# A transformer layer's feed-forward tail: where the squared norms are clamped, where the Newton steps stand, and whether TensorE takes norms or scores first

## The reference, cut to what matters

```python
q = (hidden_states @ Wq + bq).reshape(B, S, H, QD)        # 8 heads of 64
q = (q - mean) / jnp.sqrt(var + EPS_BN) * bn_gamma + bn_beta
q0 = _l2norm(q[..., :HALF])                               # x / max(|x|, 1e-12)
q1 = _l2norm(q[..., HALF:])
s0 = jnp.einsum('bshq,kq->bshk', q0, _l2norm(sub_key0))   # 32 keys
s1 = jnp.einsum('bshq,kq->bshk', q1, _l2norm(sub_key1))
ts0, ti0 = jax.lax.top_k(s0, DTK)                         # 4 of 32, twice
ts1, ti1 = jax.lax.top_k(s1, DTK)
...                                                       # 16 pairs, softmax weights w
eh = jax.nn.gelu(jnp.einsum('bshkd,bsd->bshk', expert_down[idx], hidden_states), approximate=False)
out = jnp.einsum('bshko,bshk->bso', expert_up[idx], eh * w)
```

## Time and profile before

| | |
|---|---|
| median of 3 runs | 424.44 us (423.92 to 425.02) |
| profiled execution, its own time | 424.07 us |
| span of its instructions | 422.1 us |
| PE busy | 398.3 us (94%) |
| DVE busy | 298.3 us (71%) |
| ACT busy | 239.9 us (57%) |
| POOL busy | 208.2 us (49%) |
| granted TensorE clock, mean | 0.992 |

### The profile page before, as it was taken

The page is one execution under the profiler, slowest core; times in us unless marked ns, Lnnn a source line. Parts: engine busy times, 40 slices in busy tenths (PEclk is TensorE's granted clock), DMA queues, the critical chain, the costliest instruction groups (busy, mean ns, idle before and its releaser), DMA issues. The chain is left out here.

```text
span 422.1 us, 7841 instructions
## 1 busy us (share of the span) xinstructions
PE 398.3 (94%) x2569; PEld 366.2 (87%) x2569; DVE 298.3 (71%) x1112; ACT 239.9 (57%) x527; POOL 208.2 (49%) x195
## 2 busy tenths in 40 slices
PE   2999999987999999999999999999999988999877
PEld 2788888866899999999999999998787978999866
DVE  5889677667556575475764655557595999898996
ACT  3687656314655455565554544443465878777363
POOL 2588999931814234332343312000120757989894
PEclk9999999999999999999999999999999997999999
DMA  8700222002322123212222200000000000000101
GB/s 250 263 2 2 78 77 77 6 0 78 107 79 76 53 79 101 58 50 55 78 76 58 78 2 2 0 2 1 27 0 1 2 3 1 26 27 26 39 26 62
DMA packets 19991, 21.36 MB, mean 51 GB/s; under 512 B 3180, under 2 KB 16624, under 8 KB 19952
## 3 DMA queue, kind: packets, MB, share of 16 engines
q1 hardware_dynamic: 18832, 19.96, 15.7%
q10 hardware_dynamic: 1120, 0.92, 0.8%
HBM read 18.78 MB, written 2.10 MB: 49 GB/s over the span
## 5 line engine op out<-in xcount | busy, mean ns | idle before, releaser
L971 PE MATMUL att_pA<-context_cNh,att_pTh 128*128 128x256 f32 (+1 forms) x208 | 62.6, 301 | 1.0 <-DVE att_pTl L869 1.0
L972 PE MATMUL att_pA<-context_cNl,att_pTh 128*128 128x256 f32 (+1 forms) x208 | 58.4, 281 | 0.0
L973 PE MATMUL att_pA<-context_cNh,att_pTl 128*128 128x256 f32 (+1 forms) x208 | 58.1, 279 | 0.0
L869 DVE TENSOR_TENSOR att_pTl<-att_pR,att_pTh 128x512 fp32r<-128x512 f32 x64 | 37.4, 586 | 26.7 <-ACT att_pTh L786 26.5
L1166 POOL TENSOR_TENSOR ffn_prod<-ffn_first,ffn_near 128x1024 f32<-128x1024 f32 (+1 forms) x29 | 54.2, 1887 | 2.1 <-DVE ffn_first L1559 2.1
L888 DVE TENSOR_REDUCE att_mx<-keep_pQ 128x1 f32<-128x402 f32 x64 | 35.6, 568 | 25.4 <-PE keep_pQ L77 25.3
L776 POOL TENSOR_TENSOR context_cTl<-keep_raw,context_cTh 128x512 fp32r<-128x512 f32 (+1 forms) x24 | 23.1, 981 | 47.8 <-ACT context_cTh L800 47.8
L776 POOL TENSOR_TENSOR context_cNl<-keep_raw,context_cNh 128x512 fp32r<-128x512 f32 (+1 forms) x21 | 25.1, 1211 | 41.8 <-ACT context_cNh L800 41.8
L971 PEld LDWEIGHTS att_pA<-context_cNh,att_pTh 128*128 128x128 f32 (+1 forms) x208 | 39.1, 188 | 2.2 <-DVE att_pTl L869 1.4
L972 PEld LDWEIGHTS att_pA<-context_cNl,att_pTh 128*128 128x128 f32 (+1 forms) x208 | 39.3, 189 | 0.0
L973 PEld LDWEIGHTS att_pA<-context_cNh,att_pTl 128*128 128x128 f32 (+1 forms) x208 | 39.2, 188 | 0.0
(11 more groups left out here) (302 smaller groups left out, 1153.2 us busy)
## 6 DMA issues: line engine op xcount, KB each, us to landing
keep_raw<-in_ctxT SPq DMA_DIRECT2D x24, 256.0 KB, 2.6
keep_raw<-in_ctx SPq DMA_DIRECT2D x24, 256.0 KB, 2.6
out<-keep_x SPq DMA_DIRECT2D x16, 128.0 KB, 1.7
keep_x<-in_x SPq DMA_DIRECT2D x3, 512.0 KB, 9.1
gru_wout<-in_W_out SPq DMA_DIRECT2D x1, 512.0 KB, 8.6
keep_raw<-in_fWq SPq DMA_DIRECT2D x2, 256.0 KB
keep_raw<-in_ctxT SPq DMA_DIRECT2D x8, 32.5 KB, 3.6
keep_raw<-in_ctx SPq DMA_DIRECT2D x4, 65.0 KB
```

Source lines behind the costliest of these rows:

```text
L869: dve.tensor_tensor(to, bank, half(it, 0, n)[0].bitcast(F32), ALU.subtract).then_inc(bank_free, 1)
L971: pe.matmul(pA[:, 0:D], l[0], r[0], start=(kt == 0), stop=False)
L972: pe.matmul(pA[:, 0:D], l[0], r[1], start=False, stop=False)
L973: last = pe.matmul(pA[:, 0:D], l[1], r[0], start=False, stop=(kt == CT - 1))
```

## The change

- The clamp leaves VectorE. ScalarE computes `over = Relu(n - eps^2)` from PSUM and then `nroot = Sqrt(over + eps^2)`, which is the same number. Both take their constant from a small tile (`eps2`), as a bias.
- A Sqrt of one column (`eps1`) stands ahead of the wait for TensorE's norms; the table load goes with it.
- The Newton step is written with the factor -0.5 taken into the keys (`keyT`), and the steps of batches 1 to 4 now stand between the match-replaces of `remove`: behind head 1 the reciprocal, behind heads 3, 5 and 7 the other three. Before, those of batches 1 and 2 stood behind the whole `remove` and those of 3 and 4 between MAX8.
- TensorE takes `norms` ahead of `scores` in every other pass.
- GpSimd sets the two constants at the start of the stage.

```diff
@@ gpsimd
+                for n, v in enumerate((-NORM_EPS ** 2, NORM_EPS ** 2)):
+                    pool.memset(eps2[:, n:n + 1], v).then_inc(const_ready, 1)
@@ scalar
                 def norm_roots(k):
-                    act.wait_ge(n2_ready, k + 1)
-                    m = len(BATCHES[k]) * PER * HALVES
-                    act.activation(nroot[:, 0:m], n2[:, 0:m], ACT.Sqrt).then_inc(nroot_ready, 1)
+                    m, a = len(BATCHES[k]) * PER * HALVES, BATCHES[k][0] * PER * HALVES
+                    if k == 0:
+                        act.wait_ge(const_ready, 5)
+                    act.activation(eps1[:, k:k + 1], eps2[:, 1:2], ACT.Sqrt)
+                    act.wait_ge(norm_mm, BATCHES[k][-1] + 1)
+                    if k >= 1:
+                        act.wait_ge(ninv_ready, k)
+                    act.activation(over[:, 0:m], pN[:, a:a + m], ACT.Relu, bias=eps2[:, 0:1]).then_inc(over_ready, 1)
+                    act.wait_ge(over_ready, k + 1)
+                    act.activation(nroot[:, 0:m], over[:, 0:m], ACT.Sqrt, bias=eps2[:, 1:2]).then_inc(nroot_ready, 1)
@@ vector
-                            dve.tensor_copy(keyT[:], pK[:, 0:P]).then_inc(key_ready, 1)
+                            dve.tensor_scalar(keyT[:], pK[:, 0:P], -0.5, None, ALU.mult).then_inc(key_ready, 1)
...
-                def squares(k):
-                    ...
-                    dve.wait_ge(norm_mm, BATCHES[k][-1] + 1)
-                    dve.tensor_scalar(n2[:, 0:m], pN[:, a:a + m], NORM_EPS ** 2, None, ALU.max).then_inc(n2_ready, 1)
...
-                def remove(i):
+                def remove(i, steps):
...
                         ins = dve.match_replace(picked[:, i % 2, h], top[:, n % 2, t, h, 0:2 * TOPK],
                                                 e[:, n % 2, t, h, REST:PAIR], 0.0)
+                        if h % 2 == 1:
+                            next(steps, None)
...
-                    if t == 0 and i > 2:
-                        for k in norm_batch:
-                            squares(k)
...
-                    remove(i)
-                    if i in (0, 2):
-                        for _ in inverse_norm_steps(1 if i == 0 else 2):
-                            pass
+                    remove(i, refined)
+                    for _ in refined:
+                        pass
@@ tensor
                 for i in range(TILES):
                     n, t = i // PER, i % PER
+                    if t == 0 and 3 <= n + 2 < GROUPS:
+                        norms(n + 2)
                     if 4 <= i + 2 < TILES:
                         scores(i + 2)
-                    if t == 0 and 3 <= n + 2 < GROUPS:
-                        norms(n + 2)
```

More of the change, by code:

```diff
@@ L1071, in stage_ffn @@
         sq = st.sb("sq", [P, 2, QC, COLS])
-        n2, nroot, nt, nu = (st.sb(n, [P, MOST]) for n in ("n2", "nroot", "nt", "nu"))
+        over, nroot, nt, nu = (st.sb(n, [P, MOST]) for n in ("over", "nroot", "nt", "nu"))
+        eps2, eps1 = st.sb("eps2", [P, 2]), st.sb("eps1", [P, len(BATCHES)])
         ninv = st.sb("ninv", [P, TILES, HALVES])
@@ L1110, in stage_ffn @@
         mv_ready, avg_mm, bn_ready = st.sem("mv_ready"), st.sem("avg_mm"), st.sem("bn_ready")
-        sq_ready, sq_pool, norm_mm, n2_ready, nroot_ready, ninv_ready = (
-            st.sem(n) for n in ("sq_ready", "sq_pool", "norm_mm", "n2_ready", "nroot_ready", "ninv_ready"))
+        sq_ready, sq_pool, norm_mm, over_ready, nroot_ready, ninv_ready = (
+            st.sem(n) for n in ("sq_ready", "sq_pool", "norm_mm", "over_ready", "nroot_ready", "ninv_ready"))
         q_ready_dve, q_ready_pool, q_ready_act = (st.sem(n) for n in ("q_ready_dve", "q_ready_pool", "q_ready_act"))
@@ L1196, in _ @@
                                        pattern=[[-1, P]], channel_multiplier=1).then_inc(pair_ready, 1)
-                pool.wait_ge(const_ready, 3)
+                pool.wait_ge(const_ready, 5)
                 pool.wait_ge(pair_ready, 4)
@@ L1200, in _ @@
                     pool.memset(group_of[q * HALF:(q + 1) * HALF, q:q + 1], 1.0).then_inc(const_ready, 1)
-                pool.wait_ge(const_ready, 7)
+                pool.wait_ge(const_ready, 9)
                 pool.wait_ge(bve_ready, 1)
@@ L1340, in leftover @@
                     if i == 0:
-                        act.wait_ge(const_ready, 3)
+                        act.wait_ge(const_ready, 5)
                     if n >= 2:
@@ L1476, in normed @@
                         dve.tensor_scalar(q, q, bn[:, 0:1], bn[:, 1:2], ALU.mult, ALU.add).then_inc(q_ready_dve, 1)
-                def squares(k):
-                    m = len(BATCHES[k]) * PER * HALVES
-                    a = BATCHES[k][0] * PER * HALVES
-                    dve.wait_ge(norm_mm, BATCHES[k][-1] + 1)
-                    dve.tensor_scalar(n2[:, 0:m], pN[:, a:a + m], NORM_EPS ** 2, None, ALU.max).then_inc(n2_ready, 1)
                 def inverse_norm_steps(k):
@@ L1492, in inverse_norm_steps @@
                     need(a)
-                    a = note(dve.scalar_tensor_tensor(out=t, in0=n2[:, 0:m], scalar=-0.5, in1=yy, op0=ALU.mult,
+                    a = note(dve.scalar_tensor_tensor(out=t, in0=over[:, 0:m], scalar=NORM_EPS ** 2, in1=yy, op0=ALU.add,
                                                       op1=ALU.mult))
@@ L1500, in inverse_norm_steps @@
                     to = ninv[:, BATCHES[k][0] * PER:(BATCHES[k][-1] + 1) * PER].rearrange("p t g -> p (t g)")
-                    dve.scalar_tensor_tensor(out=to, in0=u, scalar=1.5, in1=yy, op0=ALU.add,
+                    dve.scalar_tensor_tensor(out=to, in0=u, scalar=3.0, in1=yy, op0=ALU.subtract,
                                              op1=ALU.mult).then_inc(ninv_ready, 1)
@@ L1593, in _ @@
                 normed()
-                squares(0)
                 for _ in inverse_norm_steps(0):
@@ L1600, in _ @@
                     n, t = i // PER, i % PER
+                    refined = iter(())
                     if t == 0:
-                        norm_batch = [k for k in range(2, len(BATCHES)) if n + 2 == BATCHES[k][-1]]
-                        steps = itertools.chain(weight_steps(n - 1, 1 if n == 1 else 0) if n >= 1 else iter(()),
-                                                *(inverse_norm_steps(k) for k in norm_batch if i > 2))
+                        steps = weight_steps(n - 1, 1 if n == 1 else 0) if n >= 1 else iter(())
+                        for k in range(1, len(BATCHES)):
+                            if i == (0 if k == 1 else PER * (BATCHES[k][-1] - 2)):
+                                refined = inverse_norm_steps(k)
                     if i == 1:
@@ L1620, in _ @@
                     largest(i, 0, steps)
-                    if i == 0:
-                        squares(1)
                     for _ in steps:
                         pass
-                    if i == 2:
-                        squares(2)
-                    remove(i)
-                    if i in (0, 2):
-                        for _ in inverse_norm_steps(1 if i == 0 else 2):
-                            pass
+                    remove(i, refined)
+                    for _ in refined:
+                        pass
                     if i == 0:
@@ L1675, in norms @@
                     if k >= 1 and n == BATCHES[k][0]:
-                        pe.wait_ge(n2_ready, k)
+                        pe.wait_ge(over_ready, k)
                     for c in range(QC):
@@ L1717, in sum_last @@
                     pe.wait_ge(h_ready, i - 1)
-                    pe.wait_ge(n2_ready, len(BATCHES))
+                    pe.wait_ge(over_ready, len(BATCHES))
                     pe.wait_ge(part_pool, 2)
@@ L1767, in _ @@
                 expert_product(3)
-                pe.wait_ge(const_ready, 7)
+                pe.wait_ge(const_ready, 9)
                 pe.wait_ge(key_ready, 1)
```

## The result

| | before | after |
|---|---|---|
| median of 6 runs each | 424.26 us (423.86 to 425.02) | 427.04 us (425.58 to 427.83) |
| ratio, 95% interval | | 1.0047 [1.0028, 1.0066] |
| profiled execution, its own time | 424.07 us | 427.20 us |
| span of its instructions | 422.1 us | 425.3 us |
| granted TensorE clock, mean | 0.992 | 0.980 |

Run again beside three variants, it measured 1.0046 [1.0027, 1.0065]. So it is slower by 0.3 to 0.7%. The medians of the first comparison alone lie 0.66% apart, those of the second 0.44%; where this text says 0.47% it is the recorded ratio. The median is outside the likeliest case of the prediction and near the time of its second rival (427.4).

The account below looks back on a forecast made before the run. It took a serial start-up through VectorE and ScalarE, then a TensorE-bound middle, as the bound. Lag 1.97 less 0.91 and 0.83 gave +0.23 on 424.07, so 424.30, plus 0.37 for the median: 424.7 us; range 423.2 to 426.7.

Parts of the forecast that it names:

- likeliest case: Whole kernel: the summed terms hold, 424.7 us, or 423.6 to 426.3 with the unknown prices; chance 0.62.
- second rival: TensorE stays at half clock past 355.26, so norms(4) and scores(6) take 2.68 us more: 427.4 us; chance 0.13.
- Prices of the clamp, small root and biased root: ScalarE's new operations: clamp and biased root 0.32 or 0.35 us each, the one-column root 0.11.
- Batch 1: Pass 0: VectorE waits 1.25 us for ScalarE's root inside the first `remove`, and `scaled(2)` starts 0.91 later.
- Batch 2: Pass 2: ScalarE's gelu load starts at 347.02, 1.18 us later than before, and so does `sum_heads(0)`, at 350.43.
- TensorE's new order: Pass 4: norms(4), now ahead of scores(6), wait 1.15 us for ScalarE's squares; `sum_heads(1)` starts 1.97 late.
- Norms 1.77 [...], scores 0.91: Pass 4 on TensorE: norms(4) take 1.77 us, then scores(6) 0.91, so `sum_heads(1)` starts at 357.94.
- the sum: Whole kernel: lag 1.97 less 0.91 for norms' place and 0.83 for batch 4's shorter way gives +0.23 us.
- the lag: From `sum_heads(1)` on, TensorE is 1.97 us late and stays so through norms(7).
- The first rival: The lag is made up before norms(7), only the gains stand: -1.74 us, 422.7 us; chance 0.15.
- The third: ScalarE pays another 1.28 us table load in each of four batches: 429.8 us; chance 0.10, shared with other mishaps.
- dear price: ScalarE's upper bound: small root 0.23 us, clamp and root 0.49 each, adding 0.40 per batch.

Follow-up runs that it names:

- e6: The changed kernel plus dummy matmuls nobody reads: 4 between norms(2) and norms(3), 12 ahead of the gelu wait, 12 ahead of norms(4); ratio 0.9994.
- e4: The changed kernel with the steps of batches 1 and 2 behind `remove` again and norms ahead of scores only from pass 6; ratio 0.9972.
- e10: The changed kernel plus 12 dummy matmuls nobody reads, only ahead of norms(4); median 424.94 us, ratio 0.9997.

## Where the prediction was right and where wrong

- **Prices of the clamp, small root and biased root**: 0.32/0.35, 0.11 and 0.32/0.35 forecast; rows 0.27/0.30, 0.11 (335.83 to 335.94) and 0.32/0.35. Right to 0.05.
- **Batch 1**: VectorE's wait 1.25 forecast, 1.01 measured; `scaled(2)` +0.91 forecast, 338.29 + 0.12 is +0.70. The root was ready 0.06 sooner (cheaper clamp) and VectorE came to it 0.18 later, hence the shorter wait; from the reciprocal to `scaled(2)` it was 1.69 us where the terms gave 1.84.
- **Batch 2**: gelu's load at 347.02 forecast; 346.54 + 0.12 = 346.66. `sum_heads(0)` +1.18 forecast, +0.83 measured. The chain was right and 0.35 too long. TensorE's wait ahead of it was 2.66 and not 4.2, since the half clock had already slowed scores(4) and (5).
- **TensorE's new order**: norms(4) at 355.26 after 1.15 us of waiting forecast; 354.89 + 0.12 after 1.04 measured. Right.
- **The step that failed** is the next one, "Norms 1.77 [...], scores 0.91": durations at full clock, for a TensorE that had just waited twice. They were 3.40 and 1.85, and the first 1.7 us of `sum_heads(1)` ran at half clock as well. `sum_heads(1)` came at 360.14 + 0.12, not 357.94. This was the second rival, and the prediction's own sign of being wrong, a half clock past 355, came true (361.82); `near`(11) was 3.25 us from 392.15 and not within 1. The rival's price, 2.7, was near: norms(7) came at 386.63 + 0.12 against 383.63, 3.12 later, of which some 0.8 were lost in `sum_heads(1)`, whose half clock the price left out. Its chance, 0.13, was too low. The reason against it, "it came back soon after work resumed", was read from a trace in which scores(6) filled the wait that the change opens. The same working said that TensorE would wait there; the clock after that wait had to be doubted with it.
- **At full clock the forecast holds to 0.6 us**: counted from the first norms, `sum_heads(1)` was forecast at 30.01 us and `near`(11) at 64.45; e6 has 30.59 and 65.02. The 0.58 is there at norms(4) already, which stood behind the dummies and not behind the squares. Its ratio is 0.9994 [0.9974, 1.0013], which covers the 1.0005 of the sum.
- **Who carries the lag**: I let it travel through TensorE to norms(7). It travelled at once through scores(6), `scaled(6)` and `near`(5); from there GpSimd works without a break but for 0.71 every second tile.
- **The first rival** (lag made up, 422.7) happened in no run of the changed kernel. Its -1.74 is nearly reached by e4, which takes away the lag: -1.5 us in the median, -1.2 by the ratio.
- **The third** (a second table load) didn't happen: one load per batch.
- **The range**, 423.2 to 426.7: the median of 427.04 is 0.3 us outside, the time by the ratio (1.0047 x 424.26 = 426.3) inside. That it is inside is luck: the sum's own case reaches 426.3 only with every ScalarE operation at its dear price, and they came at or under the price taken, while the rival that did happen stands at 427.4, outside the range. Either is slower, to which I gave 0.28.

By ratios to before, of single edits: the order costs 0.50% on the changed kernel (1.0047 against 0.9997) and 0.21% on the one before; the steps of batches 1 and 2 cost 0.32% (1.0047 against 1.0015). They overlap, since undoing the order alone recovers all. That the order costs more behind the longer start-up is likely and not shown: the difference of 0.29% is no larger than its own uncertainty, some 0.3% by the three intervals. As to clock or waiting: e6 and e10 keep the order and fill the wait, in their traces norms(4) come no earlier for it, and no loss is left that can be told. So most of the order's cost on the changed kernel is clock; the exact split is not measured.

What stays open is what sets the phase of the clock. In two executions of equal code the clock fell at nearly the same place (16.94 and 16.77 us behind the first norms), but in one it came back only at 361.82, and in the other at 347.37, to fall again at 354.19. The Trainium skill (TensorE: Matmul & The Clock Gate, section The HAM clock gate) says that the gate's window runs free of the kernel; that equal code met two patterns agrees with it, as far as two executions can. The prediction took from that rule that the second rival could strike one execution at 427.4 and spare the next at 424.7; none of the 18 executions of the changed kernel was under 425.58.

## What to carry to other kernels

Ahead of moving work to the front of an in-order queue, ask whether its input is there; if not, the work that it overtook was filling a wait. A short wait on TensorE can cost twice: itself, and the clock of what follows it, so bound what follows by the durations at half clock too whenever the trace shows a half clock nearby. A good reordering in the steady part can be spoiled by the same order at the start: give the first passes their own, as e4 does.

## What the runs showed of the hardware

- The clock can fall while TensorE works: in the changed kernel it went to 0.50 at 344.75, with TensorE busy 4.10 of 4.10 us before it, 3.5 of them on four-column matmuls. Whether these are the cause isn't settled.
- After a wait of 1.04 us at half clock it stayed there for 6.9 us more of unbroken work (354.89 to 361.82); in the one trace with dummies in its place (e10) the clock came back 6 us sooner (355.85).
- A root in a small tile right behind a table load starts 0.01 to 0.02 us after it (334.54 + 1.28 to 335.83): nothing beyond the load's 1.28 was paid.
- Between match-replaces, an independent multiply of 32 columns costs VectorE 0.10 us (337.15 to 337.25) until the next instruction starts, instead of the 0.22 of one whose successor needs its result (331.11 to 331.33).
